# GNN layer pair on one NeuronCore: the sort's comparisons and one-hot on VectorE in instructions of two slots instead of eight

## The reference, cut to what matters

```python
# x: (12500, 128), src/dst: (412500,) int32, edge_attr_64: (412500, 64)
feat_in, feat_out = h @ W_in.T + b_in, h @ W_out.T + b_out
a_in  = seg_mean(feat_in[src],  dst, N)
a_out = seg_mean(feat_out[dst], src, N)
h1 = gru_cell(concatenate((a_in, a_out), axis=1), h)
x = layernorm(x + h1)
messages = relu(concatenate([x[row], x[col], edge_attr], -1) @ W1 + b1) @ W2 + b2
messages = messages * sigmoid(edge_attr @ Wa + ba)
x = layernorm(x + (x + segment_sum(messages, row, N)))
```

## Time and profile before

| | us |
|---|---|
| median of 3 runs | 14005.82 (14005.5 to 14013.05) |
| the profiled execution | 14025.38 |
| its span, first to last instruction | 14023.4 |
| busy: PE / DVE / ACT / POOL | 8570.3 / 7855.3 / 2750.6 / 9894.3 |
| mean granted clock of TensorE | 0.743 |

### The profile page before, as it was taken

How to read it: one execution, slowest core, us unless ns; L and a number is a source line. 1 busy time by engine, 2 the same in 40 slices (tenths; PEclk the granted TensorE clock), 3 DMA queues, 4 the chain that set the end, 5 groups by cost and what they waited for, 6 DMA issues and landing times. The chain is left out here.

```text
span 14023.4 us, 243621 instructions
## 1 busy us (share of the span) xinstructions
PE 8570.3 (61%) x53687; PEld 7649.0 (55%) x53688; DVE 7855.3 (56%) x22211; ACT 2750.6 (20%) x7304; POOL 9894.3 (71%) x10125
## 2 busy tenths in 40 slices
PE   3777775333333333333477777697777777777775
PEld 3555554333333333333377777556777777777775
DVE  6555555555555555555577777664444455444444
ACT  0000000111111111111000000053444444444444
POOL 3777775777777777777777777405777777777774
PEclk9555555555555555556688888898999999999998
DMA  5822223666666666666677777603333334333336
GB/s 182 298 54 54 54 54 85 191 190 188 189 189 190 187 190 191 188 189 190 173 184 188 184 188 185 126 27 88 79 79 79 79 86 95 80 79 80 79 80 82
DMA packets 2665576, 1884.05 MB, mean 134 GB/s; under 512 B 1375879, under 2 KB 2460455, under 8 KB 2664868
## 3 DMA queue, kind: packets, MB, share of 16 engines
q1 hardware_dynamic: 2003018, 923.76, 26.2%
q0 software_dynamic: 377360, 782.89, 19.8%
q10 hardware_dynamic: 284998, 175.59, 4.2%
HBM read 1509.53 MB, written 483.44 MB: 142 GB/s over the span
## 5 line engine op out<-in xcount | busy, mean ns | idle before, releaser
L1807 POOL DMA_INDIRECT p<-q_rows,small x3432 | 3255.8, 949 | 1659.1 <-issue 967.2
L1002 PE MATMUL bank<-p,ring 128*128 x6656 | 1548.3, 426 | 2928.3 <-DVE ring L955 2925.8
L1002 PEld LDWEIGHTS bank<-p,ring 128*128 128x128 f32 x6656 | 1437.0, 328 | 3039.5 <-issue 3039.4
L1061 POOL DMA_INDIRECT edges_a<-ring,small x1664 | 1727.8, 1038 | 592.5 <-issue 451.4
L1061 POOL DMA_INDIRECT edges_b<-ring,small x1664 | 1725.8, 1037 | 507.3 <-issue 453.4
L804 POOL DMA_INDIRECT ring<-in_x,ring x1664 | 1572.5, 945 | 533.4 <-issue 512.1
L1845 PE MATMUL bank<-ring 128*128 128x256 f32 x3432 | 1225.4, 443 | 955.1 <-DVE p L1757 954.1
L1203 POOL DMA_INDIRECT ring<-in_x,small x1352 | 1278.0, 945 | 466.8 <-issue 405.9
L836 PE MATMUL bank<-ring 128*128 128x129 f32 x3328 | 1237.7, 489 | 589.6 <-DMA ring<-in_x,ring 457.4
L1757 DVE TENSOR_TENSOR p<-bank,p 128x512 f32<-128x512 f32 x858 | 552.9, 686 | 1780.8 <-DMA p<-q_rows,small 1779.5
L1223 PE MATMUL bank<-p,ring 128*128 128x129 f32 x8360 | 1202.2, 313 | 505.7 <-DVE ring L1151 505.6
(11 more groups left out here) (284 smaller groups left out, 13662.5 us busy)
## 6 DMA issues: line engine op xcount, KB each, us to landing
p<-rows_by_slot SPq DMA_DIRECT2D x418, 928.0 KB
p<-edges_b SPq DMA_DIRECT2D x530, 262.0 KB
p<-edges_a SPq DMA_DIRECT2D x520, 262.0 KB
bonds_by_dst<-in_bond ACTq DMA_DIRECT2D x5, 20625.0 KB, 159.2
ring<-edges_b SPq DMA_DIRECT2D x1920, 33.0 KB
ring<-edges_a SPq DMA_DIRECT2D x1792, 33.0 KB
p<-q_rows,small POOLq DMA_INDIRECT x3432
ring<-bonds_by_dst ACTq DMA_DIRECT2D x1672, 32.0 KB
```

What stands on the lines that cost most here:

```text
L1002: last = nc.tensor.matmul(found[q][:, j, :], hot_t[g % GRPS][:, QUAD * h + j, :], x, start=True, stop=True, skip_group_check=True)
L1061: pool.indirect_dma_start(out=c.edges[s], out_offset=bass.IndirectOffsetOnAxis(ap=pos[:, k:k + 1], axis=0), in_=rec[:, k, :], in_offset=No ...
L1807: pool.indirect_dma_start(out=gath[g][:, k, :], out_offset=None, in_=c.q_dram, in_offset=bass.IndirectOffsetOnAxis(ap=gidx[g][:, k:k + 1], ...
```

## The change

Each of the three VectorE lines that handled eight slots in one instruction now handles two, in four instructions one after the other: the comparison with all bucket numbers (L961, which is L964 after), the one with the bucket rows (L965, L969 after) and the one-hot (L955, L956 after). Operands, types and results are the same. Each of the four increments its semaphore, so all counts that are waited for are scaled: `s_hot` by four, `s_equal` from 2 to 8 a group. No buffer, no load and no other instruction changes.

```diff
@@ sort_records, SyncE
             for n in range(2):
-                sp.wait_ge(s_hot, n + 1)
+                sp.wait_ge(s_hot, 4 * n + 4)
                 load_rows(n, n)
...
-                        sp.wait_ge(s_hot, u + 3)
+                        sp.wait_ge(s_hot, u * 4 + 12)
                         load_rows(u + 2, g % 2)
...
@@ VectorE
             def mark(n, to):
-                nc.vector.tensor_scalar(hot_t[to], locals_[n], index, None, ALU.is_equal).then_inc(s_hot, 1)
+                for k in range(0, HALF, 2):
+                    nc.vector.tensor_scalar(hot_t[to][:, k:k + 2, :], locals_[n][:, k:k + 2, :], index, None,
+                                            ALU.is_equal).then_inc(s_hot, 1)
...
-                nc.vector.tensor_tensor(equal[:, :, 0:BK], bucket.unsqueeze(2).to_broadcast([P, HALF, BK]),
-                                        c.iota[:, 0:BK].unsqueeze(1).to_broadcast([P, HALF, BK]),
-                                        ALU.is_equal).then_inc(s_equal, 1)
+                for k in range(0, HALF, 2):
+                    nc.vector.tensor_tensor(equal[:, k:k + 2, 0:BK], bucket[:, k:k + 2].unsqueeze(2).to_broadcast([P, 2, BK]),
+                                            c.iota[:, 0:BK].unsqueeze(1).to_broadcast([P, 2, BK]),
+                                            ALU.is_equal).then_inc(s_equal, 1)
                 dve.wait_ge(s_row[n], (16 * GRPS) * i + 16 * (g // 2 + 1))
-                nc.vector.tensor_tensor(equal[:, :, BK:BOTH], buckets[n],
-                                        bucket.unsqueeze(2).to_broadcast([P, HALF, P]), ALU.is_equal).then_inc(s_equal, 1)
-                dve.wait_ge(s_equal, u * 2 + 2)
+                for k in range(0, HALF, 2):
+                    nc.vector.tensor_tensor(equal[:, k:k + 2, BK:BOTH], buckets[n][:, k:k + 2, :],
+                                            bucket[:, k:k + 2].unsqueeze(2).to_broadcast([P, 2, P]),
+                                            ALU.is_equal).then_inc(s_equal, 1)
+                dve.wait_ge(s_equal, u * HALF + HALF)
...
@@ TensorE
-                    pe.wait_ge(s_hot, i * LOOK + (g + 1))
+                    pe.wait_ge(s_hot, i * (4 * LOOK) + (4 * g + 4))
```

## The result

The changed kernel took **14156.06 us** (median of 3 runs, 14151.51 to 14159.76), against 14005.82 before: a ratio of **1.0105, 95% interval 1.0082 to 1.0128**. It is 150 us slower. Forecast were 13850, with a range to 13970.

What follows compares the result with a forecast made beforehand. The prediction took sort_records to be bound by POOL's pauses and scatters, with 272 us of stretch from VectorE holds. Leaving 115 gave 157 back: 14006 - 157 = 13849, said as 13850, range 13780 to 13970.

Steps and rivals of the forecast that it cites:

- What bounds the stage: In sort_records, POOL never waits for data; the stage lasts 3328 pauses of 0.305 us plus 3328 scatters.
- VectorE's cost: In sort_records, nine added instructions' fixed parts cost VectorE 0.82 us a group, 341 us over the stage.
- What it gives back: Scatter stretch in sort_records: 115 us left of 272, so 157 us given back, bounds 126 to 212.
- a factor of 0.75 and a bound of 146 us left: Allowance for VectorE's fixed phase to POOL: at best x 0.75, 60 us of stretch left; at worst 146.
- It costs the stage nothing: VectorE idles: VectorE's added 341 us were hidden by its 2027.3 us idle ahead of L979 and about 36 us of lead.
- The bound of 0.19 us a scatter: Claimed that no piece of the three split lines can stretch a scatter by more than 0.19 us.
- a free 0.10 at every instruction's front: Scatters beginning in the first 0.10 us of a holding VectorE instruction were taken to go free.
- POOL gets in between two instructions that stand back to back: A waiting scatter comes through at the border of adjacent VectorE instructions, so a hold ends with one piece.
- The multiply and sum: The eight L974 instructions a group, unchanged, were taken to stretch scatters by 0.08 us a group before and after.
- The rival that POOL might be kept out: Four L955 pieces act as one hold of 1.17 us: 25 us saved, 13981, or nothing or small loss; chance 0.09.
- dealt out anew: Rival: more pieces hit more scatters, less than 75 us back, 13930 to 13978; chance 0.10 for over 28 back.
- VectorE's loop: Rival: VectorE's loop becomes the bound, 10.98 us a group against 10.74, 100 us slower, 14106; chance 0.05.

Runs made afterwards that it cites:

- e5_chain: The changed kernel with each piece of the three lines waiting for completion of the piece ahead; 13917.22 us, 0.9929 of the kernel before.
- e6_shift: The kernel before, nothing split, with two memsets of unused columns (about 0.53 us) ahead of L961; 14156.85 us, ratio 1.0101.
- e14_nudge: The changed kernel with one memset of 30 unused elements ahead of the compare pieces; 13968.33 us, 0.9976 of the kernel before.
- e4_onlymark: The kernel before with L955 alone split into four pieces, L961 and L965 whole; 14168.62 us, ratio 1.0104.
- e1_waits: The changed kernel with an already fulfilled wait ahead of the second to fourth piece of each line; 14152.43 us, 1.0098 of the kernel before.
- e16_chain_mark: The changed kernel with only the L955 pieces each waiting for completion of the one ahead; 13944.38 us, 0.9956 of the kernel before.
- e11_tt_split: The kernel before with both comparisons in four pieces without gaps, L955 whole; 13948.97 us, ratio 0.9956.
- e12: The kernel before with both comparisons in four pieces without gaps, L955 whole, and two memsets ahead of them; 14025.02 us, ratio 1.0013.
- e13: The kernel before with both comparisons in four pieces, L955 whole, completion waits between bucket-row pieces only; 13936.00 us, ratio 0.9952.
- e15: The kernel before with comparisons in four gapless pieces, L955 whole, and two memsets ahead totalling 14 elements less than in e12; 14025.31 us, ratio 1.0014.
- e9: The kernel before with both comparisons in four pieces, each waiting for completion of the one ahead, L955 whole; 13945.81 us, ratio 0.9948.
- e10: The kernel before with comparisons in four pieces separated by completion waits, L955 whole, and two memsets ahead; 13896.44 us, ratio 0.9925.

## Why the prediction was wrong, point by point

**What bounds the stage: right.** POOL's pause is 0.305 in every run, its idle time 1014 to 1015 us in each, and the time moved with the stretch: the change has 138 us more of it and is 150 slower, e5_chain has 88 less and is 0.7% faster.

**VectorE's cost: the sizes nearly right.** Pieces 364, 412 and 378 ns for 0.37, 0.42, 0.35. The run of L955 pieces takes 1.14 to 1.41 us, median 1.28, where I had 1.17: most pieces follow each other at 0.27 us as I had it, some at up to 0.51. VectorE's idle time stayed large, 1777 us where I had 1530 for a stage 157 us shorter.

**The step that failed** was under "What it gives back": the stretch was summed as if scatters fell anywhere, and the fixed phase, which I had seen, came in only as a factor of 0.75 and a bound of 146 us left. The runs show that the phase decides. Moving unsplit instructions by 0.5 us changes the stretch from 272 to 408 (e6_shift), and moving the split ones by some 0.04 us from 410 to 194 (e14_nudge). "It costs the stage nothing: VectorE idles" was true of waiting and false as a whole: L955's longer run shifted what came after it. The row on that was in my hands: the earlier trace rows have the scatter 0.55 into L961; with L961 some 0.5 later it begins with it, and is held for all of a whole L961 (e4_onlymark, e6_shift) or for its first piece, and the next scatter then meets the row pieces at a border. Over the traces the scatter nearest to the compare's start begins 0.51 into it before and 0.03 after (medians).

**The bound of 0.19 us a scatter was wrong.** It used a free 0.10 at every instruction's front, for which the rows shown had one scatter, and that one began ahead of L955. In the traces L955 has such a front: in every run the scatters that begin up to some 0.10 us into it or its pieces go free, later ones are held. The multiply and sum hold from 0.04 on, in every run too, and of the scatters that begin 0.01 to 0.04 into the second row piece of the changed kernel all are held, by that piece for up to 0.27 (195 scatters, 51 us) or by the rest of the run. In e6_shift, behind a memset, the compare holds even scatters that begin up to 0.02 ahead of its recorded start, while in e14_nudge, also behind a memset, those that begin 0.005 ahead go free. What sets the length of the front stays open.

**"POOL gets in between two instructions that stand back to back" was taken from a few borders as a rule, and it isn't one.** 184 scatters of the changed kernel took 1.85 to 1.95 us, held to the end of the run of row pieces; in two of 3328 a scatter waited through all pieces of both comparisons, 3.39 us. The prediction had named just this as a sign of being wrong: scatters of 1.3 us and more, a hold over several pieces. Nor are pieces needed for it: in e4_onlymark six scatters waited for the two whole comparisons, 2.98 us. The rival that POOL might be kept out was placed at L955, whose pieces hold little (5 us).

**The multiply and sum** was carried over at 0.08 us a group; it went from 38 us to 96, as more scatters fell on it. In the split kernels with L955 whole it is half of what is left.

None of the rivals was what happened, though "dealt out anew" has the right idea: it said that the phase might settle so that POOL runs into the pieces, and was priced as a gain all the same, by the bound of 0.19. VectorE's loop did not become the bound, and the slower side was priced only through it.

**What stays open**: which scatters a run without gaps holds to its end. It was seen with L955 in pieces (184 scatters; in e1_waits more; 34 in e16_chain_mark; 6 over two whole comparisons in e4_onlymark) and almost never with L955 whole (3 in e11_tt_split, none in e12, e13 and e15); but e14_nudge has L955's pieces and none. Neither the run of L955 pieces nor the phase at the border explains it alone; most cases, not all, have both. The scatters that waited through both comparisons (two in the changed kernel, five in e1_waits, six in e4_onlymark) all began 0 to 0.015 us into the compare. A completed piece ahead of each ended it wherever it was tried (e5, e9, e10, and e13 for the row pieces), at phases that differ from the changed kernel's, so the gap itself as the cause is argued, not shown.

## What to carry to other kernels

Where one engine never waits and its instructions are stretched by another's, more work on the other is not free though that one idles: draw both timelines, move the second by the time that is added, and read off what each instruction now meets, before any mean is taken. Price a bound on a hold from the worst row at a border, and if instructions are cut so that others may come between them, leave a real gap, a wait for the completion of the piece ahead; it cost VectorE about 1 us a group, and no scatter was held beyond one piece at the three phases tried (stretch 184, 182 and 149 us). Such a result should be tried with a small fill ahead of the work: 30 elements of memset took the changed kernel from 14156 to 13968 us.

## What the runs showed of the hardware that was not expected

- A stretched scatter ends 0.83 us after the end of the VectorE instruction that held it, in every run. How far into the instruction a scatter may begin and still go free differs by instruction: some 0.10 us for L955, whole or in pieces, and 0.04 for the multiply and sum, the same in every run; the compare of e6_shift, behind a memset, had none. For a tensor_scalar into fp32 (L955) there is the late hold too, 0.12.
- Two VectorE instructions with both inputs in SBUF, back to back, can keep a waiting scatter out together: up to 3.40 us for 0.96 in pieces, 2.99 for two whole ones (e4_onlymark). A fulfilled semaphore wait between them makes no difference (404 us of stretch for 410); with a wait for the completion of the one ahead there is no such hold (184), at another phase.
- The memsets (464 elements 0.45 us, 100 elements 0.14) held no scatter: in e6_shift all but three of the stretched scatters are accounted for by the ends of other instructions.
- Four L955 pieces of 256 elements take 1.14 to 1.41 us in a run in the changed kernel, median 1.28, single pieces 0.33 to 0.59, while the comparisons' pieces vary by 0.07 at most.
